# A megakernel with a Mamba-2 layer and a mixture of experts: the order of work within the steps of its pipelined stage, on five engines

## What is computed

```python
# tokenizer: conv over 9 taps, scaled by the window's norm, tanh, bias, relu -> 32 x 248 x 128
h = relu(tanh(conv(x) * scale) + bias)
# Mamba-2: 4 heads of 64, state 64, conv of 4 taps
zxbcdt = layernorm(h) @ in_proj_w
xBC = silu(conv4(xBC) + conv_b);  dt = softplus(dt + dt_bias);  decay = exp(dt * A)
# per step: state = decay * state + dt * x (outer) B;  y = state . C;  y += D_skip * x
y = y * silu(z);  y = y * rsqrt(mean(y * y) + EPS) * norm_w
h = h + y @ out_proj_w
# mixture of experts: 16 experts, top 2, a shared branch, and a feed-forward behind it
g = layer_norm(layernorm(h));  gate = softmax((g @ router_w + router_b) / 0.7);  top_k(gate, 2)
moe = sum of the two chosen experts' silu(g @ w1 + b1) @ w2 + b2, weighted
moe = moe + 0.25 * (silu(g @ sw1 + sb1) @ sw2 + sb2)
out = layernorm(h) + moe + silu(layer_norm(moe) @ ff_w1 + ff_b1) @ ff_w2 + ff_b2   # and the residual
```

## Time and profile before

| | us |
|---|---|
| median of 3 runs | 1109.16 (1107.78 to 1111.79) |
| the profiled execution | 1112.74 |
| its span | 1111.0 |
| TensorE busy | 948.3 (85%) |
| VectorE busy | 746.7 (67%) |
| GpSimd busy | 572.2 (51%) |
| ScalarE busy | 441.8 (40%) |

### The profile page before, as it was taken

One profiled execution on the slowest core, in us unless ns is written; L12 is line 12 of the kernel. 1 busy time (PEld: TensorE's weight loads), 2 busy tenths in 40 slices (PEclk: granted clock), 3 DMA queues, 4 the chain that ended last, 5 costly groups with the idle time before them and its releaser, 6 DMA issues. The chain is left out here.

```text
span 1111.0 us, 22688 instructions
## 1 busy us (share of the span) xinstructions
PE 948.3 (85%) x6371; PEld 795.0 (72%) x6372; DVE 746.7 (67%) x2288; ACT 441.8 (40%) x1068; POOL 572.2 (51%) x531
## 2 busy tenths in 40 slices
PE   0499999999999999999887429999999999388887
PEld 0377877877777777778665229999999999266665
DVE  4348779788797797978866615555555555488884
ACT  3233443343433333423322215555555555144443
POOL 3044444665676556775655735555555555243342
PEclk9899999999999999999986659999999999699999
DMA  6400000000000000000036422222222221223331
GB/s 134 104 20 10 1 10 11 29 20 22 17 29 29 22 24 12 29 20 17 12 95 201 137 69 61 55 63 60 63 66 62 66 62 49 74 56 91 92 92 37
DMA packets 71868, 58.97 MB, mean 53 GB/s; under 512 B 18992, under 2 KB 61291, under 8 KB 71808
## 3 DMA queue, kind: packets, MB, share of 16 engines
q1 hardware_dynamic: 63264, 41.88, 14.4%
q0 software_dynamic: 8544, 16.34, 4.4%
HBM read 35.62 MB, written 23.81 MB: 53 GB/s over the span
## 5 line engine op out<-in xcount | busy, mean ns | idle before, releaser
L1429 POOL DMA_INDIRECT y_tokens<-arena x139 | 155.9, 1122 | 144.7 <-DVE arena L1452 111.3
L1416 ACT ACTIVATE arena<-psum,arena 128x128 f32<-128x128 f32 x556 | 158.6, 368 | 132.0 <-PE psum L1390 130.8
L1390 PE MATMUL psum<-arena 128*128 128x128 f32 x1112 | 155.9, 284 | 3.5 <-DVE arena L1447 1.2
L1390 PEld LDWEIGHTS psum<-arena 128*128 128x128 f32 x1112 | 137.1, 194 | 16.2 <-issue 8.3
L1403 PE MATMUL psum<-arena 128*128 x1112 | 147.8, 275 | 0.4 <-ACT arena L1416 0.4
L1043 POOL DMA_INDIRECT x_slots<-arena,idx x128 | 127.3, 994 | 35.9 <-issue 35.9
L1444 DVE COPY arena<-arena 128x644 f32 x139 | 69.3, 499 | 109.5 <-DVE arena L1452 89.8
L1403 PEld LDWEIGHTS psum<-arena 128*128 128x128 f32 x1112 | 136.0, 193 | 0.6 <-issue 0.6
L623 PE MATMUL psum<-hnT_hi,w_tap_hi 128*128 128x496 f32 x192 | 80.3, 418 | 0.0
L1152 DVE TENSOR_TENSOR_SCAN arena<-psum,arena 124x496 f32<-124x496 f32 x64 | 72.4, 1173 | 6.7 <-PE psum L736 6.7
L624 PE MATMUL psum<-hnT_lo,w_tap_hi 128*128 128x496 f32 x192 | 75.8, 395 | 0.0
(11 more groups left out here) (249 smaller groups left out, 2051.2 us busy)
## 6 DMA issues: line engine op xcount, KB each, us to landing
arena<-x_slots SPq DMA_DIRECT2D x139, 64.5 KB
arena<-y_tokens SPq DMA_DIRECT2D x16, 448.0 KB
arena<-in_x SPq DMA_DIRECT2D x16, 256.0 KB, 2.9
out_tokens<-arena SPq DMA_DIRECT2D x16, 224.0 KB
arena<-in_ew SPq DMA_DIRECT2D x1, 2304.0 KB
y_tokens<-arena POOLq DMA_INDIRECT x139
x_slots<-zero_src SPq DMA_DIRECT2D x33, 64.5 KB, 2.7
arena<-in_x SPq DMA_DIRECT2D x4, 512.0 KB, 6.7
```

Source lines behind the costliest of these rows:

```text
L1390: last = nc.tensor.matmul(psum[:, 2 + b.q % 2, k * 128:(k + 1) * 128], w1_blk[b.q % 4][:, k * 128:(k + 1) * 128], hT[b.q % 2], start=True, ...
L1416: last = nc.scalar.activation(EHT[t.q % 2][:, k * 128:(k + 1) * 128], psum[:, 2 + t.q % 2, k * 128:(k + 1) * 128], ACT.Silu, bias=w1_blk[t ...
L1429: nc.gpsimd.indirect_dma_start(out=y_tokens, out_offset=bass.IndirectOffsetOnAxis(ap=xb[t.q][:, F:F + 1].bitcast(i32), axis=0), in_=YO[t.q ...
```

## The change

Five edits, all of them to the order of calls within a step:

1. TensorE: at a step's start decays(c, 0) comes ahead of scores(c, 0).
2. TensorE: output(c) moves behind shared_down(d) and hn_transposes(a), to the step's end. VectorE: shared_out(d) and hn_rest(a) move ahead of sum_squares, mean_squares and residual of unit c.
3. ScalarE: silu(b, 2) moves ahead of square(c, 0), while silu(b, 3) stays behind it.
4. ScalarE: hnT_copy(a) moves ahead of residual_input(d).
5. GpSimd: for units below 11, the scatters of u for j = 0 and 1, four DMAs that stood behind rs8_of(c), are split: two go ahead of rr_of(c), two between rr_of(c) and rs8_of(c). The last units' scatters keep their places.

```diff
@@ TensorE
-                    if c is not None: scores(c, 0); decays(c, 0)
+                    if c is not None: decays(c, 0); scores(c, 0)
...
                     if b is not None: projection(b, 4, d)
-                    if c is not None: output(c)
                     if d is not None: shared_down(d, a, b)
                     if a is not None: hn_transposes(a, d, t)
+                    if c is not None: output(c)
@@ ScalarE
                     if a is not None: tanh(a); relu(a)
+                    if b is not None: silu(b, 2)
                     if c is not None: square(c, 0)
-                    if b is not None: silu(b, 2); silu(b, 3)
+                    if b is not None: silu(b, 3)
                     if d is not None: shared_silu(d)
                     if c is not None: square(c, 1)
                     if b is not None: silu(b, 4)
+                    if a is not None: hnT_copy(a)
                     if d is not None: residual_input(d)
-                    if a is not None: hnT_copy(a)
@@ GpSimd
                     a, b, c, u, v = at(t, 0), at(t, 1), at(t, 2), at(t, 5), at(t, 6)
+                    early = u is not None and u < UNITS - 5
...
                     if c == UNITS - 1: scatter(UNITS - 4, (0, 1))
+                    if early: scatter(u, (0,))
                     if c is not None: rr_of(c)
                     if c == UNITS - 1: scatter(UNITS - 4, (2,))
+                    if early: scatter(u, (1,))
                     if c is not None: rs8_of(c)
-                    if u is not None and u < UNITS - 5: scatter(u, (0, 1))
                     if u == UNITS - 5: scatter(u, range(4))
@@ VectorE
-                    if c is not None: sum_squares(c); mean_squares(c); residual(c)
                     if d is not None: shared_out(d)
                     if a is not None: hn_rest(a)
+                    if c is not None: sum_squares(c); mean_squares(c); residual(c)
                     if c is not None: new_stats(c)
```

## The result

The changed kernel takes 1118.76 us in the median of seven runs (1117.6 to 1122.59) for 1109.16 of the kernel before beside it (seven runs, 1107.78 to 1113.48). The ratio is 1.0084, with a 95% interval of 1.0062 to 1.0106. The profiled execution took 1117.6 with a span of 1115.8. The executions of the kernel before lie in two groups, in the largest comparison eleven at 1107.9 to 1110.4 us with a granted clock of 0.949 to 0.953 and ten at 1112.8 to 1114.6 with 0.941 to 0.944, and the profiled one (1112.74, 0.944) is one of the slower group.

What follows compares the result with a forecast made beforehand. VectorE was taken to bound the routed steps and TensorE the plain ones. To the median of 1109.2 us, +6.2 from the steps and +4.2 from clock falls gave 1119.5, own range 1115 to 1123, 8 in 10 within 1107 to 1124.

Steps and rivals of the forecast that it cites:

- Output behind the shared product: Behind each step's mark: scans at +9.38 for +7.92, convolution at +13.80 with a 1.5 us pause, plain steps 33.04.
- Silu ahead of the square: Before x_rows in plain steps: the 2.1 us pause goes, since silu(b, 2) then needs only projection(b, 2).
- The scatters cost nothing where they went: GpSimd idles some 3.7 us before rr_of, likewise before rs8_of; two scatters take 2.55, so moving them there is free.
- Collision: Routed steps: GpSimd's bias add meets VectorE's dt_rest in all of them, costing VectorE 1.1 us; routed steps take 35.62.
- Ten steps: Steps t = 6 to 15: 343.3 us for 340.87, +2.4, with clock falls counted apart at +4.2.
- t = 2 to 5: Pipeline start: +1.86 us up to the mark of t = 4, then -0.2 in t = 5.
- t = 16: Step 16: scans at +9.38 for +8.23 behind the mark, +1.15 us with nothing hiding it.
- t = 17: Step 17: +1.45 us at its start, -0.4 at its end, where new_stats comes earlier.
- The total: Whole kernel: 1109.2 plus 6.2 of steps plus 4.2 of clock gives 1119.5 us.
- The collision did come: Rival, chance 0.18: the bias add misses dt_rest, five later routed steps are 1.05 us shorter each, total 1110.7.
- TensorE is held by the late scans: Opposed rival, chance 0.11: x_rest comes in time for the convolution, 12 us less, 1097; half of that gives 1103.
- Not all pauses were followed by the lower clock: Opposed rival, chance 0.09: all six pauses bring the lower clock at 1.66 us each, total 1125 to 1128.

Runs made afterwards that it cites:

- e1: The kernel before with only the output products' move on TensorE and the matching moves on VectorE and ScalarE: 1134.0 us, ratio 1.0211 to the kernel before.
- e2: The changed kernel with the output and its matching VectorE and ScalarE calls back in their old places: 1107.73 us, ratio 0.9974 to the kernel before.
- e8: The kernel before with only silu(b, 2) moved ahead of square(c, 0): 1121.07 us for 1126.86 of the kernel before, ratio 0.9935.
- e7: The changed kernel with x_scale(b) ahead of norm(a) on VectorE: 1136.6 us for 1126.86 of the kernel before, ratio 1.0072.
- e5: The kernel before with decays ahead of scores, silu(b, 2) ahead of the square, scatters split in odd steps only: 1113.71 us for 1126.86, ratio 0.987.
- r2: The changed kernel run and traced once more on a third chip: 1119.13 us for 1109.23 of the kernel before, ratio 1.0084.
- e6: The kernel before with decays first, silu(b, 2) ahead of the square, odd-step scatter split, x_scale(b) ahead of norm(a): 1108.2 us for 1126.86, ratio 0.9842.
- r1: Repeat on a third chip of the old-output-place kernel with odd-step scatter split and x_scale(b) ahead of norm(a): 1094.34 us for 1109.23, ratio 0.9872.
- e4: The changed kernel with scatters split in odd steps only, in even steps all four behind rs8_of: 1112.68 us, ratio 1.0019 to the kernel before.
- e3: The changed kernel with its scatters put back behind rs8_of: 1118.7 us, ratio 1.0072 to the kernel before.

## Why the prediction was right, step by step

- **Output behind the shared product.** Right, and the part that decides: the scans at +9.32 (forecast +9.38), the convolution at +13.74 (+13.80) with a wait of 1.3 to 1.4 in every step (1.5), plain steps of 33.15 to 33.20 (33.04). e1 shows it alone and e2 its absence.
- **Silu ahead of the square.** Right for the changed kernel. The text gave the whole pause of the plain steps to the Silu's place; e8 shows that this is worth only half (0.95 us of pause stay), and that the scatters moved out of the plain steps' front are needed for the other. What the text left out is that ScalarE's relu stands ahead of the Silu and waits for the bias add, which comes behind GpSimd's scatters.
- **The scatters cost nothing where they went.** Right in the steps: the residual waits 1.16 for GpSimd's power, 1.12 before.
- **Collision.** Right, 1.2 us at L1130 in each routed step (1.37 for 0.176), and by e7 not bound to that one instruction. Routed steps 35.63, forecast 35.62. This was the forecast's most doubtful step, since it hung on two starts; they came 0.02 us apart.
- **Ten steps.** 347.39 measured. The sum had 343.3 plus 4.2 of clock, 347.5, against the trace of before that it used. Two of six pauses were followed by the lower clock (steps 9 and 15), one of them in the second trace of the changed kernel; I took two to three.
- **t = 2 to 5.** The mark of step 5 came 200.74 - 197.45 = 3.29 us later for the +1.66 that I had. Of that, 0.94 is there already at x_rows of step 2 (93.41 for 92.47), ahead of all that the sum counted. Between the convolutions of steps 1 and 2 it is 82.34 - 60.79 = 21.55 for 81.41 - 60.59 = 20.82, so 0.73 of it arises there, and this is edit 1, of which the prediction says that the order of decays and scores changes nothing: at the start of step 2 the decays (L736), now first, wait for x_scale, where before they came behind the scores and waited for nothing. The rest is 0.21 that stands there before. Of what follows, 0.79 more than the sum's 1.86 lies up to the mark of step 4, most of it in the first convolution behind a column sum, which came 0.95 later where I had 0.4; step 5 took 0.30 less, 0.1 more than the 0.2 of the sum.

The decays of step 2 after the change (the row of before is 75.34, 1.06 us long and with no wait):

```profile
75.27 1.06 PE L736 MATMUL psum<-ident,arena 124*124 124x124 f32 x8 [0.49 <-DVE arena L1145]
```

The other traces bear it out: the stretch is 21.5 in e2 to e5 and r2, which have edit 1, and 20.8 in e1 and e8, which haven't, and in e6, e7 and r1, where x_scale comes ahead of norm and is done in time.

- **t = 16.** Wrong in sign: 32.84 for 34.77, where I had +1.15. Before, TensorE had the lower clock in a part of that step (0.85 in the mean), after, less of it (0.95). The scans' delay did come, 9.32 for 8.23 behind the mark, and the transposes of hh (L783) with it, 15.86 for 14.78. But they hardly lengthened the step, where the prediction has "nothing hides it". In the trace of before without the lower clock in this step, TensorE still waits 2.68 us for the Silu ahead of x_rows (561.75 above). After the change it waits for nothing there: the later transposes and a stretch at the lower clock behind them have used up that time, and x_rows stands 25.72 behind the mark for 25.66 in that trace. The step is 32.84 for 32.65, so +0.2 where the sum had +1.15. Which edits let the Silu come early enough, no run tells apart.
- **t = 17.** Mis-sized. I had +1.05; from the mark of step 16 to rs8_of(15) it is 619.63 - 580.97 = 38.66 for 614.21 - 573.09 = 41.12, so 2.5 less. Part of the reason is the clock again: the output product of unit 15 took 3.77 us at the lower clock before and takes 2.01 now. The amount changes from execution to execution: the second trace of the changed kernel has 621.06 - 580.52 = 40.54 here. Part of that gain is lost again to a queue that I hadn't named: the unchanged four scatters of unit 12 stand on GpSimd ahead of rr_of, and now it is they that hold the residual.

GpSimd and VectorE at that place:

```profile
614.74 0.98 POOL L1044 DMA_INDIRECT x_slots<-arena,idx  x1 [0.30 <-issue]
615.72 1.06 POOL L1027 TENSOR_TENSOR arena<-arena,minus_half 124x4 f32<-124x4 f32 x1
...
616.82 1.13 DVE L1201 SCALAR_TENSOR_TENSOR Hb<-psum,arena,Hb 124x128 f32<-124x128 f32 x4 [3.07 <-POOL arena L1027]
```

- **The total.** The spans of the first two traces differ by 3.29 + 6.52 (steps 6 to 15) - 1.93 (t = 16) - 2.46 (to rs8_of) + 0.51 (from there to the first loads of the next stage, 661.71 and 655.78) - 1.13 (the stages behind) = +4.8. The forecast had +10.3 over the median and the medians came out +9.6. The two agree so well because the trace of before that I added to was itself 3.6 us over its median, with more of the lower clock than the faster executions: a forecast against the faster trace, with one fall in steps 6 to 15 in place of two, would have had more of the output's cost and less of the clock's. The mechanism and the sizes of the steps were right; that the sum met the median to 0.7 us is in part luck.
- **Rivals.** The collision did come; its absence, in e4, gives 1112.7 (the rival had 1110.7). TensorE is held by the late scans. That rival's sum of 12 us starts from the mean of all ten steps; from the plain ones alone, 172.8 us before, it would be 172.8 - 5 x 31.64 = 14.6. Not all pauses were followed by the lower clock in the changed kernel.

## What to carry over

When a product is moved behind others on one engine, count the chain that hangs on it on the other engines up to the engine itself: here a move that leaves TensorE's work the same made a wait of 1.3 us in every step, since column sums, power, residual and scans stand between the output and the next convolution. A gain that opens room on one engine (scatters out of a step's front) also moves what follows on that engine; look what it will now stand beside, and if it is a collision, do the edit only in the steps where it isn't one (e5 against e2: 1.1 us a step). Before a single trace is used as the base of a sum, ask how many of its stretches at the lower clock an execution near the median would have.

## What was unexpected of the hardware

Equal pauses of TensorE had unequal ends. Of the six pauses of 2.0 to 2.2 us ahead of x_rows the lower clock followed three, three and one in the three traces of the kernel before (twice the same three), two and one in the changed kernel, three in e2 and one in e7; in e1 it followed all five that the plain steps have. Behind the 0.9 to 1.1 us pauses ahead of x_rows in e3, e4, e5, e6 and e8 it never came in the steps 6 to 15. A second pause ahead in the same step is not what decides: in e1 the convolution waits 1.1 us some 14 us ahead of the pause, and all five fell, while in the changed kernel it waits 1.3 some 15 us ahead, and two and one of six fell. Nor is a long pause needed: in step 5 of e1 and in step 7 of e4 (granted clock 0.90 in both) the clock was lower from shortly behind the column sums, and since the convolution of the step before TensorE had waited for nothing longer than 0.25 us. In e4 that was:

```profile
239.46 1.03 PE L768 MATMUL psum<-ones_col,arena 128*124 128x1 f32 x8 [0.21 <-DVE arena L1189]
```

The steps around these two have the same products and waits there and kept their clock. What decides, no run here shows.

And norm's tensor_scalar instructions, with all operands in the local memory, took 2.05 us beside GpSimd's gate and 1.14 away from it, while x_scale, which reads one operand from PSUM, took 1.21 in both places.
